# The second and third layer norm written by ScalarE as product plus offset, in a four-block transformer kernel

## What is computed

```
x = x + tanh(g_xattn[0]) * align(ctx, layernorm(x))            # norm 0
x = x + tanh(g_ffn[0])   * moe64(layernorm(x), router_w, ...)  # norm 1
x = x + tanh(g_xattn[1]) * cross_attn(layernorm(x), ctx, ...)  # norm 2
x = x + tanh(g_ffn[1])   * moe8(layernorm(x), gate_w, ...)     # norm 3

def _layernorm(x, axis=-1, eps=1e-05):
    m = jnp.mean(x, axis=axis, keepdims=True)
    v = jnp.var(x, axis=axis, keepdims=True)
    return (x - m) / jnp.sqrt(v + eps)
```

## Time and profile before

| | |
|---|---|
| time, median of 3 runs | 828.75 us (828.06 to 835.66) |
| profiled execution, its own time | 828.82 us |
| its span in the trace | 827.1 us |
| PE busy | 677.6 us, 82% of the span |
| DVE busy | 629.6 us, 76% |
| ACT busy | 412.1 us, 50% |
| POOL busy | 413.5 us, 50% |
| norm 1, first `update` to last `low` | 166.4 to 183.6 us |
| norm 2, first `update` to last DVE `query` | 469.3 to 489.6 us |

### The profile page before, as it was taken

The page is one execution under the profiler, slowest core; times in us unless marked ns, Lnnn a source line. Parts: engine busy times, 40 slices in busy tenths (PEclk is TensorE's granted clock), DMA queues, the critical chain, the costliest instruction groups (busy, mean ns, idle before and its releaser), DMA issues.

```text
span 827.1 us, 13197 instructions
## 1 busy us (share of the span) xinstructions
PE 677.6 (82%) x3114; PEld 541.0 (65%) x3114; DVE 629.6 (76%) x2089; ACT 412.1 (50%) x755; POOL 413.5 (50%) x449
## 2 busy tenths in 40 slices
PE   4423310089999999999999869999998999999996
PEld 2211110077888888888888649998866888888884
DVE  7699999688777777777777786777786777777774
ACT  3524300034565656565656555444545656565563
POOL 6377730036666666666666441110145666666663
PEclk9655555558999999999999969999699999999999
DMA  5555421125776867767777100000417756666661
GB/s 135 78 122 143 135 72 33 36 51 121 158 153 138 163 132 163 135 157 144 157 144 151 41 10 1 1 0 0 103 41 149 165 133 159 142 152 149 150 142 52
DMA packets 79209, 89.14 MB, mean 108 GB/s; under 512 B 44181, under 2 KB 56838, under 8 KB 75716
## 3 DMA queue, kind: packets, MB, share of 16 engines
q1 hardware_dynamic: 72118, 78.37, 44.8%
q0 software_dynamic: 4320, 9.68, 3.8%
q10 hardware_dynamic: 2734, 0.69, 0.4%
HBM read 79.84 MB, written 8.70 MB: 107 GB/s over the span
## 4 chain that ended last, share of the span: by engine, by line
PE 72%; DVE 19%; issue 4%; DMA 2%; ACT 2%; POOL 1%; DVEq 0%; POOLq 0%; ACTq 0%
PE bank L1011 14%; PE bank L1013 14%; PE bank L1012 14%; PE bank L1147 7%; PE bank L1145 6%; PE bank L1144 6%; PE bank L1075 4%; DVE arena L1439 3%; PE bank L1057 2%; DVE arena L1435 2%; DVE arena L1396 2%; DVE arena L1388 1%; DVE arena L1436 1%; DVE arena L1397 1%; PE bank L950 1%
## 5 line engine op out<-in xcount | busy, mean ns | idle before, releaser
L702 POOL TENSOR_TENSOR act_lo<-arena,act_hi 128x512 fp32r<-128x512 f32 x232 | 300.2, 1294 | 199.3 <-ACT act_hi L842 199.3
L1651 DVE TENSOR_TENSOR bank<-arena,bank 128x512 f32<-128x512 f32 x232 | 160.7, 693 | 103.8 <-PE bank L1013 71.7
L854 ACT ACTIVATE arena<-bank 128x512 f32<-128x512 f32 x232 | 138.9, 599 | 177.5 <-PE bank L1013 175.3
L1011 PE MATMUL bank<-xn_hi,w_hi 128*128 128x512 f32 x464 | 186.7, 402 | 3.1 <-DVE arena L1659 3.1
L1013 PE MATMUL bank<-xn_lo,w_hi 128*128 128x512 f32 x464 | 184.6, 398 | 0.0
L1012 PE MATMUL bank<-xn_hi,w_lo 128*128 128x512 f32 x464 | 184.1, 397 | 0.0
L1659 DVE TENSOR_TENSOR arena<-bank,arena 128x512 f32<-128x512 f32 x232 | 160.4, 691 | 20.4 <-DVE bank L1651 9.2
L842 ACT ACTIVATE act_hi<-arena 128x512 fp32r<-128x512 f32 x232 | 145.2, 626 | 13.8 <-DVE arena L1659 13.6
L1011 PEld LDWEIGHTS bank<-xn_hi,w_hi 128*128 128x128 f32 x464 | 88.3, 190 | 26.6 <-DVE arena L1659 4.6
L1013 PEld LDWEIGHTS bank<-xn_lo,w_hi 128*128 128x128 f32 x464 | 88.2, 190 | 21.8
L1012 PEld LDWEIGHTS bank<-xn_hi,w_lo 128*128 128x128 f32 x464 | 88.5, 191 | 20.8
(11 more groups left out here) (195 smaller groups left out, 958.8 us busy)
## 6 DMA issues: line engine op xcount, KB each, us to landing
arena<-scr_mask SPq DMA_DIRECT2D x94, 512.0 KB, 6.6
scr_w<-prep_out POOLq DMA_DIRECT2D x25, 192.0 KB, 2.2
w_raw<-scr_w SPq DMA_DIRECT2D x25, 192.0 KB, 6.5
arena<-scr_one SPq DMA_DIRECT2D x6, 512.0 KB, 5.6
w_raw<-in_L_ffn_expert_gate_k SPq DMA_DIRECT2D x32, 64.0 KB, 6.0
w_raw<-in_L_ffn_expert_up_k SPq DMA_DIRECT2D x32, 64.0 KB, 5.7
w_raw<-in_L_ffn_expert_down_k SPq DMA_DIRECT2D x64, 32.0 KB, 5.4
prep_in<-in_L_ffn_wg POOLq DMA_DIRECT2D x21, 64.0 KB, 2.3
```

Of the source, the lines that this page charges most:

```text
L702: nc.gpsimd.tensor_tensor(act_lo[:, k % 2, :], act_a[:, k % 2, :], act_hi[:, k % 2, :].bitcast(F32), ALU.subtract).then_inc(FF[f]["alo"], 1)
L854: nc.scalar.activation(act_s[:, k % 2, :], ps[4 + k % 2][:], ACT.Silu).then_inc(FF[f]["silu"], 1)
L1011: nc.tensor.matmul(out, w_h, x_h, start=start, stop=False)
L1651: nc.vector.tensor_tensor(ps[6 + i][:], act_s[:, i, :], ps[6 + i][:], ALU.mult).then_inc(FF[f]["t"], 1)
```

## The change

In norms 1 and 2 `xn` is written by ACT alone, all four tiles of a batch, as Identity(x * rstd + offset). DVE makes `offset` = -mean * rstd for a batch in one more small step (L1345 of the changed kernel) and no longer writes `xn` there; POOL doesn't either and keeps its two `low`. Norms 0 and 3 keep the old way. A new semaphore `s_xna` counts ACT's tiles; PE's transposes and POOL's first bias addition wait on it. ACT's program is reordered: in the round of batch b it does `root(b)`, `normalise(b-1)`, `high(b-2)` and, in norm 2, `query(b-3)`.

```
+            def normalise(k, b):                      # ACT
+                act.wait_ge(s_rstd, B * k + b + 1)
+                for t in range(TPB * b, TPB * (b + 1)):
+                    nc.scalar.activation(xn[:, t, :], x_res[:, t, :], ACT.Identity, bias=offset[:, t:t + 1],
+                                         scale=rstd[:, 3, t:t + 1]).then_inc(s_xna, 1)
...
                     if b >= 1:                        # ACT norm(k), k > 0
-                        high(k, b - 1)
-                    if k == 2 and b >= 2:
-                        query(b - 2)
+                        normalise(k, b - 1)
+                    if b >= 2:
+                        high(k, b - 2)
+                    if k == 2 and b >= 3:
+                        query(b - 3)
+                if k > 0:
+                    normalise(k, B - 1)
+                    high(k, B - 2)
+                if k == 2:
+                    query(B - 3)
...
-                        nc.vector.scalar_tensor_tensor(rstd[:, 3, old], rstd[:, 2, old], 1.5, rstd[:, 0, old],
-                                                       ALU.add, ALU.mult).then_inc(s_rstd, 1)
+                        r3 = nc.vector.scalar_tensor_tensor(rstd[:, 3, old], rstd[:, 2, old], 1.5, rstd[:, 0, old],
+                                                            ALU.add, ALU.mult)
...
-                    if p >= 0:
+                    if p >= 0 and k > 0:
+                        after(r3)
+                        nc.vector.scalar_tensor_tensor(offset[:, old], mv[:, old, 0], -1.0, rstd[:, 3, old],
+                                                       ALU.mult, ALU.mult).then_inc(s_rstd, 1)
+                    if p >= 0 and k == 0:
                         normalise(k, p)
...
             def norm(k):                              # POOL
-                for b in range(B + 1):
-                    if b < B:
+                for b in range(B):
+                    if k in (0, 3):
                         normalise(k, b)
-                    if k in (1, 2) and 1 <= b <= POOL_LOW:
-                        low(k, b - 1)
+                    elif b < POOL_LOW:
+                        low(k, b)
```

More of the change, by code:

```diff
@@ L126, in program @@
         rstd = sb("rstd", [P, 4, TILES])
+        offset = sb("offset", [P, TILES])
         ident = sb("ident", [P, P])
@@ L324, in program @@
         s_xnp = sem("xn_ready_pool")
+        s_xna = sem("xn_ready_act")
         s_xt = sem("xn_transposed")
@@ L672, in tile @@
                         pool.wait_ge(s_gbo, 1)
-                        pool.wait_ge(s_xn, 3 * B * ND)
+                        pool.wait_ge(s_xna, 2 * B * TPB)
                     xi = x_res[:].rearrange("p t h -> p (t h)")[:, tok]
@@ L762, in norm @@
                         context()
+                    if k == 0:
+                        if b >= 1:
+                            high(k, b - 1)
+                        continue
                     if b >= 1:
-                        high(k, b - 1)
-                    if k == 2 and b >= 2:
-                        query(b - 2)
+                        normalise(k, b - 1)
[8 more added lines that the diff above has]
+                    query(B - 3)
                 if k in (0, 2):
@@ L945, in turn @@
                     t = TPB * b + q
-                    if q < ND:
-                        pe.wait_ge(s_xn, (B * k + b) * ND + q + 1)
+                    if k in (1, 2):
+                        pe.wait_ge(s_xna, (B * (k - 1) + b) * TPB + q + 1)
+                    elif q < ND:
+                        pe.wait_ge(s_xn, (B * (k // 3) + b) * ND + q + 1)
                     else:
-                        pe.wait_ge(s_xnp, (B * k + b) * (TPB - ND) + q - ND + 1)
+                        pe.wait_ge(s_xnp, (B * (k // 3) + b) * (TPB - ND) + q - ND + 1)
                     mm = nc.tensor.transpose(turn_bank(k, b)[:, P * q:P * (q + 1)], xn[:, t, :], ident[:])
@@ L1311, in norm @@
                         after(r2)
-                        nc.vector.scalar_tensor_tensor(rstd[:, 3, old], rstd[:, 2, old], 1.5, rstd[:, 0, old],
-                                                       ALU.add, ALU.mult).then_inc(s_rstd, 1)
+                        r3 = nc.vector.scalar_tensor_tensor(rstd[:, 3, old], rstd[:, 2, old], 1.5, rstd[:, 0, old],
+                                                            ALU.add, ALU.mult)
+                        if k == 0:
+                            r3.then_inc(s_rstd, 1)
+                        else:
+                            r3 = done(r3)
                     if b < B:
```

## The result

The changed kernel takes 836.94 us, median of 4 runs (835.12 to 838.02), beside 828.66 us for the kernel before on the same chip (4 runs, 828.06 to 835.66). The ratio is 1.0073 with a 95% interval of 1.0037 to 1.0108, so it is slower by some 3 to 9 us. The profiled execution took 837.97 us with a span of 835.9; that of before, 828.82 with a span of 827.1. The forecast was 833.4 with a range of 829.5 to 836.5. The sign was right, the size too small: the median lies 0.4 us above the upper end of the range, and the lower part of its interval lies inside it.

The account below looks back on a forecast made before the run. The prediction took DVE to pace norms 1 and 2 before the change and ACT to pace norm 1 after it. It added 1.3 us (norm 1) and 3.3 (norm 2) to 828.82, giving 833.4 us, range 829.5 to 836.5.

Parts of the forecast that it names:

- The sign: Whole kernel: the change makes it slower, 833.4 us against the profiled 828.82.
- ACT's tile: Norms 1 and 2: one 128x128 tile with two pointers lasts 472 ns and costs 0.38 us of ACT.
- the sum: Whole kernel: 1.3 us lost in norm 1 plus 3.3 in norm 2, 4.6 us on 828.82.
- DVE's rounds: Norms 1 and 2: without `xn`, with one small step, a DVE round shrinks from 3.08 to 2.37 us.
- ACT keeps pace: Rival, norms 1 and 2: three rounds in each get 0.71 us shorter, giving 824.5 us; 5%.
- Norm 1, +1.3: Norm 1: ACT becomes the pace, `high` 2 starts at 180.11 instead of 178.82, so 1.3 us later.
- The one step locked out by POOL's `low`: Norm 1: DVE's next two-input step sits out `low` 0; last `offset` at about 178.0, hidden ahead of 178.59.
- Norm 2, +3.3: Norm 2: batch 3's reciprocal queues behind DVE's `query` 0; last `query` at 492.1 against 488.80, 3.3 us later.
- The forecast's 2.6: Norm 2: the loss if PE's last passes run at the upper clock level, instead of 3.3 us.
- Behind this … keep their programs, waits and lengths: Attention's rounds, feed-forward layers, norm 3 and norm 0: unchanged, only weight split and first scores start later; nothing added.
- The rival on PE's clock: First scores and first feed-forward products: ACT's pauses keep PE's clock low, 2 to 4 us more, 835.5 to 838; 15%.

Follow-up runs that it names:

- Experiment 3: Changed kernel with DVE's `query` 0 in norm 2 moved behind the last offset; 835.07 us, ratio 1.0053 to the kernel before.
- experiment 5: The kernel before, unchanged, run and profiled a second time; 830.06 us.
- experiment 1: The change in norm 1 only, norm 2 as in the kernel before; 835.39 us, ratio 1.0046 to the kernel before.
- 2: The change in norm 2 only, norm 1 as in the kernel before; 836.17 us, ratio 1.0074 to the kernel before.
- 6: The changed kernel, unaltered, run and profiled a second time; 837.59 us.
- 7: Changed kernel, but in norms 1 and 2 DVE writes two tiles, ACT two, POOL none, with ACT's old order; 838.23 us, ratio 1.0102 to the kernel before.
- 8: The two-and-two tile split of 7 with DVE's `query` 0 in norm 2 behind the last offset; 837.88 us, ratio 1.0077 to the kernel before.
- 11: The split of 7 with POOL's `low` waiting until DVE has written its tiles of the next batch; 835.72 us, ratio 1.0058 to the kernel before.
- Experiment 9: Changed kernel with a 2.6 us delay (four awaited DVE memsets) behind norm 2's last `query`; 838.38 us, ratio 1.0103 to the kernel before.
- experiment 4: Kernel before with a 5.2 us delay (eight awaited DVE memsets) behind norm 2's last `query`; 838.45 us, ratio 1.0105 to the kernel before.
- 12: Kernel before with DVE's `query` 0 in norm 2 moved behind the tiles of batch 3; 831.18 us, ratio 1.0012 to the kernel before.
- 10: Kernel before with a 1.3 us delay (two awaited DVE memsets) behind norm 2's last `query`; 836.53 us, ratio 1.0079 to the kernel before.

## Why the prediction was right in its sign and too small in its size

**ACT's tile: right.** Forecast 0.38 us of ACT; four take 1.63 to 1.65, started 0.38 to 0.39 apart. That two pointers cost twice one was the assumption. (472 ns less the 0.10 of overlap is 0.37, not the 0.38 that the sum used; the slip was on the right side.) By the figures of the Trainium skill, page "ScalarE: Activation LUTs", section "What ACT_TABLE_LOAD costs", the estimate for one tile was 479 ns; the trace has 481.

**DVE's rounds: right.** Forecast 2.37, measured 2.32. The rounds did get shorter, and norm 1 still got longer, so the rival "ACT keeps pace" is out; it needed a tile of 0.32 us.

**Norm 1, +1.3: right.** +1.20, with `high` 2 at 180.22 where 180.11 was forecast, and the last offset done at 178.15 where 178.0 was. The one step locked out by POOL's `low` was hidden, as forecast.

**Norm 2, +3.3: right.** +3.43 between the two profiles, with the steps in the order forecast: DVE idle for 4.21, ACT for 1.82, lower clock in the last passes. `query` 0 came at 484.85 where 483.1 was forecast in the frame of before; the difference of 1.75 is the later start of the norm (471.04 against 469.28), the 1.2 of norm 1 among it. Experiment 3 gives the queue alone 2.60, more than its wait of 1.82 on ACT; in part this goes with the clock of the last products (0.50 against 0.72 in 485 to 490). The forecast's 2.6 was for last passes at the upper level in both kernels. With the lower level in both, which is what experiment 5 offers as the kernel before, the loss is 2.7.

**"Behind this … keep their programs, waits and lengths": this step failed.** They kept programs and waits but not lengths. The sum had 4.6, and the two norms did take 4.6 (1.20 and 3.43). 3.5 us came at the end of the attention, some 98 us behind ACT's last tile, because TensorE's clock fell to 0.50 as the last round began instead of behind it. The rival on PE's clock had the kind of loss (products at the lower level) and the size (2 to 4 us on top, 835.5 to 838; measured 836.94), but the wrong place and reason: it looked for pauses that keep the clock low at the first scores and the first feed-forward products. Before and after differ by only 0.14 in the attention ahead of the tail and by 0.39 in the feed-forward layer ahead of norm 2, and ahead of the fall PE had hardly paused (busy for 3.08 of the 3.40 us from 583.0 to 586.4, at 1.00). That its size fits is luck, and it had only 15%.

**What of the tail is shown, and what is open.** In the profiles, the kernels with ACT's tiles and no added delay had the long tail in 8 of 8 (after, 1, 2, 3, 6, 7, 8, 11), those without ACT's tiles in 0 of 5. Experiment 9 shows that the tiles alone don't do it, since with them and 2.6 us of delay the tail is short. Nor does a later arrival, counted from the start of the span: the last-but-one group starts at 580.00 (experiment 1) with the long tail and at 580.06 (experiment 5) with the short one, and at 587.13 (experiment 4) with the short one again.

Counted from the moment at which the clock had fallen in norm 2 (476.1 before, 477.3 after), the arrival does sort all 14 profiles. The last-but-one group starts behind that fall by:

| us | tail | profiles |
|---|---|---|
| 101.8 to 102.4 | short | before, 5, 12 |
| 102.9 to 103.5 | long | 1, 3, 7, 8, 11 |
| 104.8 | short | 10 |
| 106.3 to 106.6 | long | after, 2, 6 |
| 108.4 to 109.0 | short | 4, 9 |

So what sorts them is when the work arrives relative to the clock's own earlier changes, which the changed norms shift and a delay shifts too; by this the long tail of the changed kernel is where its delay happens to land. These bands were read off afterwards and no run was made to test them, so this is a reading and not shown.

The executions without a profile warn as well. The kernel before ran 52 times beside the experiments. In 32 of them its mean granted clock was 0.879 or more and the time 828.4 to 831.0 us; in 20 the clock was 0.873 to 0.877 and the time 830.6 to 836.3. Both of its profiles are of the first kind, so "0 of 5" doesn't say that it never has the long tail. The mean clock doesn't tell the tail either: experiments 4, 9 and 10 had the short one at 0.874, 0.872 and 0.875. How much of the 3.5 us a measurement of many executions would charge to the change is therefore open; the interval of the ratio (3 to 9 us) holds both 4.6 and 8.1.

## What to carry to other kernels

When work is moved to an engine with a low busy share, add up that engine's round in the stretch where the work lands: ACT was half idle over the program and the bound in norm 1. Then look for a consumer that waits in program order ahead of the step which feeds the moved work (here DVE's `query` 0 ahead of the last reciprocal): it cost 2.6 us in norm 2, where the tiles cost 1.2 in norm 1. Moving such a step helps only where the chain to the end runs through it: in experiments 8 and 12 it brought nothing. And don't take an unchanged stretch with a nearly full PE to keep its length when what is ahead of it shifts: check in a second and third profile whether the clock falls at the same instruction.

## What the runs showed of the hardware

- The granted clock of TensorE falls at the end of the attention in every profile, but at an instruction that differs: 2.4 to 3.0 us behind the start of the last-but-one group of sixteen products in eight profiles, 6.8 to 7.9 behind it in six. Ahead of the earlier fall PE was busy for 3.08 of 3.40 us in the changed kernel, ahead of the later one for 2.30 of 2.30 in the kernel before, both at 1.00. The earlier fall costs 3.2 to 3.7 us. A delay of 2.6 us ahead of the attention moved one kernel from the first to the second.
- DVE's tile operation with one SBUF tile in and one out (128x128, x2) stood still beside POOL's two-input subtraction, 1.43 us for 0.60, not only its two-input steps (1.03 and 1.12 for 0.15 here). Beside POOL's one-input tile of 0.89 us it did not: three in 1.00 us.
- ACT's product plus offset with both operands per partition is 481 ns for 128x128 in the mean of 32, the shortest 477 and the longest 493.
